# Sandwich layer on eight cores: scores with a 65th row instead of a separate subtraction, K of both heads in rows 0 to 63, and the second LN2 moved

## The chip, the cores and the metric

The program runs on all 8 NeuronCores of one Trainium2 chip, each core on its own half of a sequence. The time is the device time of the slowest core in microseconds (us). TensorE (PE) has two clock levels here, 1.2 and 2.4 GHz; the trace gives the level that was granted as a share of full speed (0.50 or 1.00, a mean in between). DVE is VectorE, ACT is ScalarE, POOL is GpSimd, SP is SyncE, whose queue issues DMAs; PSUM is the memory that PE writes.

## What is computed

One layer of 1024 features on 4 sequences of 4096 tokens: `x = x + LN(attention(LN(x)))`, then `x = x + LN(ffn(LN(x)))`. The attention has 16 heads of 64; q is layer-normalised over all features before it is split into heads, and q is added to the attention's output:

```python
q = layer_norm(x @ Wq + bq, ln_g, ln_b);  k = x @ Wk + bk;  v = x @ Wv + bv
qk = (q * d ** -0.5) . k ;  gmax = max over all keys
out = sum(exp(qk - gmax) v) / (1e-08 + sum(exp(qk - gmax)))      # per head, in key chunks
out = (out + q) @ Wo + bo

h = silu((x @ w1.T) * s1) * ((x @ w2.T) * s2)     # 1024 -> 4096
h = gelu((h @ h1.T) * sh1);  h = gelu((h @ h2.T) * sh2)          # 4096 -> 4096, twice
return (h @ w3.T) * s3                                           # 4096 -> 1024
```

## The kernel before

Each core holds the 4096 tokens of its sequence as keys and 2048 of them as queries. Features lie on partitions, tokens along the free axis. Work is issued in program order on each engine; a small planner (`Prog`) turns declared reads and writes of named buffers into semaphore waits. A buffer name covers a whole tile, so a read waits for the last writer of any part of it.

**A1, A2** (lines 423 to 466) normalise x and project and normalise q. `emit_stats` (386) makes mean and variance with matmuls against ones into the PSUM banks psP1a and psP1b, fed by DVE casts and squares.

**Attention** (648 to 656) loops over 8 head pairs `hp`. `emit_kv` (486) loads two weight slices, makes K for both heads (L506: 8 token chunks of 512, 8 matmuls of 128x128 by 128x512 each; head 0 on partitions 0 to 63, head 1 on 64 to 127) and V (L518, 32 chunks). PSUM banks are dealt out in turn from six slots. Then come 4 query tiles of 512. For each tile, *pass 1* finds the maximum of the scores over all keys for each query: `pass1_steps` makes a list of 68 small steps. Per group of 128 queries (`qs`) there are 16 steps, each one matmul (L539, 64 rows, 512 keys) and one DVE maximum over it (L546), with the bank chosen by the key segment, psP1a for even and psP1b for odd ones, so that the two heads of a segment share a bank. A 17th step reduces the 8 maxima of each head (L554, L557), transposes them on PE (L560) and copies two rows, for head 0 to partition 0 and for head 1 to partition 64 of `grow` (L564, L567).

*Pass 2* (`emit_pass2`, 573) goes over 32 key chunks `kc` of 128. In PE's order each chunk has: the scores of both heads (L595, a pair of 64-row matmuls at tile positions (0, 0) and (64, 0)), the subtraction of the maximum (L602, a pair of 1-row matmuls of -1 by `grow`, accumulated on top), and PV of the chunk before (L582, 65 columns of weights: 64 of V and a column of ones that yields the sum of exponentials). ACT takes exp of both heads at once (L610). Behind that, two steps of pass 1 of the *next* tile are popped. The PSUM banks of scores alternate between psST0 and psST1. After 32 chunks DVE takes two reciprocals (L618, L620), PE spreads them (L622, L625), DVE multiplies and adds q; then the steps that are left over follow. In the last tile of a head pair nothing is popped.

**After attention** the output projection and its LayerNorm (661 to 688) store x1 to DRAM. **FFN** (723 to 864) takes two blocks of 1024 tokens: LN2 of two halves of 512 (L727 load, stats, L734, L736 apply), S1 (w1, w2, silu, product on DVE at L789), h1 and h2 (L811), w3 (L839), final LayerNorm (L855 to L859) and store (L861).

Of the kernel before, what the change touches and what calls it, by code (L numbers as in the profile page):

```python
# [10 lines left out]
AF = mybir.ActivationFunctionType  # L11
# [212 lines left out]
def build_program(cfg):  # L224
# [34 lines left out]
    with stack:  # L259
# [35 lines left out]

        def slot():
            h, lo, b = _slots[_si[0] % len(_slots)]
            _si[0] += 1
            return h[:, lo:lo + 512], b
# [8 lines left out]
        sem_bv = p.dma_sem("bv")  # L308
        sem_big = p.dma_sem("big")
# [27 lines left out]
        o_grow = _o_ws + 4096  # L337
# [16 lines left out]
        b_grow = [p.buf("grow0"), p.buf("grow1")]  # L354
# [31 lines left out]
        def emit_stats(bf_chunks):  # L386
            n = len(bf_chunks)
            for i, (kind, xap, xbufs) in enumerate(bf_chunks):
                if kind == "f32":
                    dst, db = sc16[i % 2], b_sc16[i % 2]  # L390
                    p.op("vector", lambda v, xap=xap, dst=dst: v.tensor_copy(  # L391
                        dst[:, :], xap), reads=list(xbufs), writes=[db], tag="cast")
                    xap, xbufs = dst[:, :], [db]
                sq, bsq = sc16[2 + (i % 2)], b_sc16[2 + (i % 2)]
                p.op("vector", lambda v, xap=xap, sq=sq: v.tensor_mul(sq[:, :], xap, xap),
                     reads=list(xbufs), writes=[bsq], tag="sq")
# [26 lines left out]
        for tc in range(NTC_F if not cfg.get("skip_a1") else 0):  # L423
# [19 lines left out]
            sem_w[0], writes=[b_ws, b_wsV, b_xbs[0], b_xbs[1]] + b_pt + b_grow, tag="wq")  # L443
# [24 lines left out]
        if cfg.get("stop_after_A2"):  # L468
# [3 lines left out]
                              o_pt=o_pt, o_grow=o_grow, o_sc=o_sc, o_ws=o_ws,  # L472
# [8 lines left out]

        kvK = [PB.view(o_ws + i * 128, 128) for i in range(ND)]
# [3 lines left out]
        def emit_kv(hp):  # L486
# [16 lines left out]
            for tc in range(NTC_F):  # L503
                ps, bps = slot()
                for i in range(ND):
                    p.op("tensor", lambda t, i=i, tc=tc, ps=ps: t.matmul(  # L506
                        ps, kvK[i][:, :], xln[i][:, tc * 512:(tc + 1) * 512],
                        start=(i == 0), stop=(i == ND - 1)),
                        reads=[b_ws, b_xln[i]], writes=[bps], war_free=(i > 0), tag="kMM")
                p.op("scalar", lambda s, tc=tc, hp=hp, ps=ps: s.activation(  # L510
                    K_hp[:, tc * 512:(tc + 1) * 512], ps, AF.Identity,
                    bias=bks_t[:, hp:hp + 1], scale=0.125),
                    reads=[bps, bbks], writes=[b_k], tag="kevac")
# [14 lines left out]

        def pass1_steps(hp, qt):
# [3 lines left out]
            steps = []  # L533
            for qs in range(4):
                for seg in range(NSEG):
                    for h in range(2):
                        def th(qs=qs, h=h, seg=seg):
                            pa, pb = (psP1a, bP1a) if (seg % 2 == 0) else (psP1b, bP1b)
                            p.op("tensor", lambda t: t.matmul(  # L539
                                pa[:, :], q_s[c][h * 64:h * 64 + 64,  # L540
                                                 t0 + qs * 128:t0 + (qs + 1) * 128],
                                K_hp[h * 64:h * 64 + 64, seg * 512:(seg + 1) * 512],
                                start=True, stop=True),
                                reads=[b_qs[c], b_k], writes=[pb], tag="s1MM")
# [6 lines left out]
                def th2(qs=qs):  # L551
                    gc0 = o_gc + gsl * 128
                    base = o_cm + gsl * 64 + qs * 16
                    p.op("vector", lambda v: v.reduce_max(  # L554
                        PF.view(gc0, 1), PF.view(base, NSEG), axis=AX.X),
                        reads=[b_cm[gsl]], writes=[b_gc[gsl], b_big1], tag="gA")
                    p.op("vector", lambda v: v.reduce_max(  # L557
                        PF.view(gc0 + 64, 1), PF.view(base + 8, NSEG), axis=AX.X),
                        reads=[b_cm[gsl]], writes=[b_gc[gsl]], tag="gB")
                    p.op("tensor", lambda t: t.transpose(  # L560
                        psP1a[0:65, 0:128], PF.view(gc0, 65), idm_t[:, :]),
                        reads=[b_gc[gsl], bidm], writes=[bP1a], tag="gT")
# [10 lines left out]
        def emit_pass2(hp, qt, nxt):  # L573
# [3 lines left out]
            g0 = o_grow + gsl * 512  # L577
# [12 lines left out]
            for kc in range(NKC):  # L590
# [3 lines left out]
                for h in range(2):  # L594
                    p.op("tensor", lambda t, kc=kc, h=h, pst=pst: t.matmul(  # L595
                        pst[:, h * 512:(h + 1) * 512],
                        K_hp[h * 64:h * 64 + 64, kc * 128:(kc + 1) * 128],
                        q_s[c][h * 64:h * 64 + 64, t0:t0 + 512],
                        start=True, stop=False, tile_position=(h * 64, 0)),
                        reads=[b_k, b_qs[c]], writes=[bsth[h]], tag="stMM")  # L600
                for h in range(2):
                    p.op("tensor", lambda t, h=h, pst=pst: t.matmul(  # L602
# [349 lines left out]
```

How the kernel before makes its waits and increments, by code:

```python
            def body(eng):  # L164
                watermark = {}
                for o in prog.ops[e]:
                    for d in o.deps:
                        if d[0] == "eng":
                            sem = prog.sems[d[1]]
                            val = prog.ops[d[1]][d[2]].sem_val
                            assert val is not None, (d, o.tag)
                        else:
                            sem = d[1].handle
                            val = d[2]
                        key = id(sem)
                        if watermark.get(key, -1) >= val:
                            continue
                        watermark[key] = val
                        eng.wait_ge(sem, val)
                    inst = o.fn(eng)
                    if o.dma_sem is not None:
                        inst.then_inc(o.dma_sem.handle, 16)
                    elif o.inc:
                        inst.then_inc(prog.sems[e], 1)
```

## Time and profile before

| | |
|---|---|
| two timed runs, median | 8107.11 us (8105.29 to 8108.93) |
| profiled execution, time | 8104.53 us |
| its span (first to last instruction, slowest core) | 8103.0 us |
| spans of all cores | 8084.3 to 8103.0 us |
| mean granted clock, cores | 0.688 to 0.691 |
| busy: PE, DVE, ACT, POOL | 5975.2, 2603.2, 1565.0, 641.9 us |
| chain that ended last, by engine | PE 70%, DVE 19%, issue 6%, DMA 3% |

The page is of one profiled execution on the slowest core. Busy times are sums over instructions; PE's are modelled, and overlapping matmuls count together, so the start times of neighbouring matmuls say more than their durations. "x2" in a row of the order of time means that two instructions were merged. In brackets stands how long the engine had been idle before, and whose result ended the wait.

### The profile page before, as it was taken

The page shows a single profiled execution, that of the slowest core. Times are in us where ns is not written, and L with a number is a line of the kernel's source. Part 1 is how long each engine was busy: PE and PEld are TensorE (multiplying, and loading weights), DVE is VectorE, ACT ScalarE, POOL GpSimd, SP SyncE. Part 2 cuts the span into 40 slices and gives each one's busy share as a digit, 9 for nine tenths or more (in the row PEclk, how much of TensorE's full clock was granted, in tenths as well). Part 3 has the DMA queues.
Part 4 walks back from the last instruction along what each step waited for, and adds up shares of the span by engine and source line. Part 5 has one row for each costly group of instructions (what it writes and reads, how often), then busy time and mean ns, then how long its engine had stood idle before and what let it go on. Part 6 is the DMA issues. An engine that isn't in the chain of part 4 may idle for free.

```text
span 8103.0 us, 82459 instructions; the slowest of 8 cores (8084.3 to 8103.0 us)
## 1 busy us (share of the span) xinstructions
PE 5975.2 (74%) x23184; PEld 1921.5 (24%) x23184; DVE 2603.2 (32%) x4355; ACT 1565.0 (19%) x1761; POOL 641.9 (8%) x737
## 2 busy tenths in 40 slices
PE   2456757857757667677677577469999967999995
PEld 0111111211211211111111111124444423444442
DVE  7544344344344344344344443620000023000002
ACT  0212312312212222122122123122001002210000
POOL 0000000000000000000000000001222220122222
PEclk6755555555555555555555555779999988999998
DMA  3100000000000000000000000256877884687888
GB/s 43 13 3 0 1 3 0 2 2 1 3 0 0 3 0 0 3 0 1 3 0 0 11 1 0 79 85 71 79 77 75 80 104 83 73 77 75 78 79 99
DMA packets 781102, 265.62 MB, mean 33 GB/s; under 512 B 684008, under 2 KB 758128, under 8 KB 780656
## 3 DMA queue, kind: packets, MB, share of 16 engines
q0 software_dynamic: 759408, 218.18, 26.7%
q1 hardware_dynamic: 21248, 42.17, 1.5%
q8 instruction: 197, 3.23, 0.2%
q14 instruction: 249, 2.04, 0.1%
HBM read 461.67 MB, written 16.78 MB: 59 GB/s over the span
## 4 chain that ended last, share of the span: by engine, by line
PE 70%; DVE 19%; issue 6%; DMA 3%; ACT 1%; DVEq 1%; POOL 0%; ACTq 0%; POOLq 0%; SPq 0%
PE psST L811 15%; DVE PF L546 10%; PE psPVa L582 7%; PE psST L602 7%; PE psST L595 5%; PE psP1a L539 5%; PE psPVb L582 5%; PE psP1b L539 5%; PE psP1a L811 4%; PE psP1b L811 4%; PE psST L764 2%; PE psST L757 2%; DMA PB<-w3t 2%; PE psST L839 1%; DVE PF L620 1%
## 5 line engine op out<-in xcount | busy, mean ns | idle before, releaser
L610 ACT ACTIVATE PB<-psST 128x1024 bf16<-128x1024 f32 x1024 | 1048.6, 1024 | 3260.3 <-PE psST L602 3259.6
L811 PE MATMUL psST<-PB 128*128 128x512 bf16 x5504 | 1199.4, 380 | 18.1 <-DMA PB<-h1t 18.1
L546 DVE TENSOR_REDUCE PF<-psP1a 128x1 f32<-128x512 f32 x1024 | 708.0, 691 | 927.9 <-PE psP1a L539 364.5
L539 PE MATMUL psP1b<-PB 64*128 64x512 bf16 x1024 | 600.9, 587 | 534.5 <-DVE PF L546 531.1
L546 DVE TENSOR_REDUCE PF<-psP1b 128x1 f32<-128x512 f32 x1024 | 708.1, 692 | 857.7 <-PE psP1b L539 420.8
L539 PE MATMUL psP1a<-PB 64*128 64x512 bf16 x1024 | 598.2, 584 | 497.2 <-DVE PF L546 409.4
L595 PE MATMUL psST<-PB 64*128 64x512 bf16 x2048 | 796.2, 611 | 0.0
L391 DVE CAST PB<-PF 128x512 bf16<-128x512 f32 x128 | 54.9, 429 | 2233.7 <-ACT PF L845 2077.4
L811 PEld LDWEIGHTS psST<-PB 128*128 128x128 bf16 x5504 | 539.6, 98 | 671.0 <-issue 24.4
L582 PE MATMUL psPVa<-PB 128*65 128x512 bf16 x1024 | 644.3, 629 | 5.2 <-ACT PB L610 5.2
L582 PE MATMUL psPVb<-PB 128*65 128x512 bf16 x1024 | 639.1, 624 | 0.0
L602 PE MATMUL psST<-PB,neg_b 1*128 1x512 bf16 x2048 | 615.6, 598 | 10.3 <-DVE PB L567 10.3
L539 PEld LDWEIGHTS psP1b<-PB 64*128 64x128 bf16 x1024 | 102.7, 100 | 994.4 <-issue 994.4
L539 PEld LDWEIGHTS psP1a<-PB 64*128 64x128 bf16 x1024 | 102.6, 100 | 992.8 <-issue 992.4
L818 ACT ACTIVATE PB<-psST,ccol_t 128x512 bf16<-128x512 f32 x172 | 118.3, 688 | 1054.3 <-PE psST L811 1054.2
L811 PE MATMUL psP1a<-PB 128*128 128x512 bf16 x1344 | 296.9, 379 | 0.0
L811 PE MATMUL psP1b<-PB 128*128 128x512 bf16 x1344 | 296.9, 379 | 0.0
L488 POOL DMA_DIRECT2D PB<-wk x8 | 7.0, 876 | 3591.8 <-PE psST L518 1738.8
L602 PEld LDWEIGHTS psST<-PB,neg_b 1*128 1x128 bf16 x2048 | 105.1, 99 | 734.8 <-issue 734.8
L618 DVE RECIPROCAL PF<-psPVa 1x512 f32<-1x512 f32 x32 | 107.4, 3355 | 534.2 <-PE psPVa L582 531.4
L801 POOL DMA_DIRECT2D PB<-h1t x256 | 224.4, 896 | 687.2 <-PE psST L811 421.2
L801 POOL DMA_DIRECT2D PB<-h2t x256 | 224.5, 896 | 659.6 <-PE psST L811 433.1
(129 smaller groups left out, 4435.0 us busy)
## 6 DMA issues: line engine op xcount, KB each, us to landing
PB<-h1t POOLq DMA_DIRECT2D x256, 256.0 KB, 5.8
PB<-h2t POOLq DMA_DIRECT2D x256, 256.0 KB, 5.7
PB<-w3t POOLq DMA_DIRECT2D x128, 256.0 KB, 6.6
PB<-w1t POOLq DMA_DIRECT2D x32, 512.0 KB, 6.2
PB<-w2t POOLq DMA_DIRECT2D x32, 512.0 KB, 8.3
PF<-x1d SPq DMA_DIRECT2D x8, 2048.0 KB, 8.7
PB<-xT POOLq DMA_DIRECT2D x8, 1024.0 KB, 12.0
PF<-xT SPq DMA_DIRECT2D x4, 2048.0 KB, 8.9
```

The costliest lines, as they stand in the source:

```text
L539: p.op("tensor", lambda t: t.matmul(pa[:, :], q_s[c][h * 64:h * 64 + 64, t0 + qs * 128:t0 + (qs + 1) * 128], K_hp[h * 64:h * 64 + 64, seg ...
L546: p.op("vector", lambda v: v.reduce_max(PF.view(col, 1), pa[:, :], axis=AX.X), reads=[pb], writes=[b_cm[gsl], b_big1], tag="s1max")
L582: p.op("tensor", lambda t, kc=kc, h=h, par=par, psv=psv: t.matmul(psv[:, :], V_hp[kc][:, h * 65:h * 65 + 65], PB.t[:, o_pt + par * 1024 + ...
L595: p.op("tensor", lambda t, kc=kc, h=h, pst=pst: t.matmul(pst[:, h * 512:(h + 1) * 512], K_hp[h * 64:h * 64 + 64, kc * 128:(kc + 1) * 128], ...
L602: p.op("tensor", lambda t, h=h, pst=pst: t.matmul(pst[:, h * 512:(h + 1) * 512], neg_b[h * 64:h * 64 + 1, :], PB.t[h * 64:h * 64 + 1, g0:g ...
L610: p.op("scalar", lambda s, par=par, pst=pst: s.activation(PB.t[:, o_pt + par * 1024:o_pt + (par + 1) * 1024], pst[:, :], AF.Exp), reads=bs ...
L618: p.op("vector", lambda v: v.reciprocal(rd[:, 0:512], psPVa[64:65, :]), reads=[bPVa], writes=[b_rd, b_big1], tag="recipA")
L757: p.op("tensor", lambda t, i=i, jj=jj, sb=sb, psa=psa, wi=wi: t.matmul(psa, fsl[wi][:, i * 256 + jj * 128:i * 256 + (jj + 1) * 128], xln2[ ...
L764: p.op("tensor", lambda t, i=i, jj=jj, sb=sb, psb2=psb2, wi=wi: t.matmul(psb2, fsl[2 + wi][:, i * 256 + jj * 128:i * 256 + (jj + 1) * 128] ...
L801: p.dma("gpsimd", lambda g, j2=j2, wi=wi, wt_d=wt_d, jq0=jq0: g.dma_start(PB.view(o_ws + wi * 4096 + jq0 * 128, NJ * 32).rearrange("p (n o ...
L811: p.op("tensor", lambda t, j=j, sb=sb, ps=ps, wi=wi, src=src: t.matmul(ps, PB.view(o_ws + wi * 4096 + j * 128, 128), src[j][:, sb * 512:(s ...
L818: bdst=bdst: s.activation(dst[j2][:, sb * 512:(sb + 1) * 512], ps, AF.Gelu, bias=0.0, scale=cc(scn, j2)),
```

## The change

- **K per head.** The K projection makes 64 columns per matmul group, once per head, and both results lie on partitions 0 to 63: head 0 in `K_hp`, head 1 in two free pieces of the slab (`kb1`, `kb2`). Row 64 of all three is set to 1.0 once.
- **Queries per head.** A first step `th0` of pass 1 copies the 512 queries of head 0 on DVE and moves those of head 1 by a DMA on SP's queue from partitions 64 to 127 to 0 to 63, into tiles `qgv`. The DMA waits for the copy, because both write the buffer `b_qg`.
- **Maximum as a 65th row.** The maxima are stored negated in row 64 of `qgv`. The scores become one 65-row matmul per head, without a tile position; the subtraction matmuls go. Matmuls of pass 1 read rows 0 to 63 for both heads.
- **Transpose step.** It has, per head, a reduction, a transpose and a one-row copy; both heads use the same column of `gc`, head 0 the bank psP1a and head 1 psP1b.
- **LN2 and slots.** LN2 of the second block is emitted behind S1 of the first block, ahead of h1. In the FFN the slots are the four halves of psST0 and psST1.

```diff
...
             for tc in range(NTC_F):
+                for h in range(2):
+                    ps, bps = slot()
+                    for i in range(ND):
+                        p.op("tensor", lambda t, i=i, tc=tc, h=h, ps=ps: t.matmul(
+                            ps[0:64, :], kvK[i][:, h * 64:(h + 1) * 64],
+                            xln[i][:, tc * 512:(tc + 1) * 512],
+                            start=(i == 0), stop=(i == ND - 1)),
...
+            def th0():
+                p.op("vector", lambda v: v.tensor_copy(
+                    qgv[gsl * 2 + 0][0:64, :], q_s[c][0:64, t0:t0 + 512]),
+                    reads=[b_qs[c]], writes=[b_qg[gsl]], tag="qgA")
+                p.dma("sync", lambda sy: sy.dma_start(
+                    qgv[gsl * 2 + 1][0:64, :], q_s[c][64:128, t0:t0 + 512]),
+                    sem_qg[gsl], reads=[b_qs[c]], writes=[b_qg[gsl]], tag="qgB")
+            steps.append(th0)
...
-                                pa[:, :], q_s[c][h * 64:h * 64 + 64,
-                                                 t0 + qs * 128:t0 + (qs + 1) * 128],
-                                K_hp[h * 64:h * 64 + 64, seg * 512:(seg + 1) * 512],
+                                pa[:, :],
+                                qgv[gsl * 2 + h][0:64, qs * 128:(qs + 1) * 128],
+                                rhs, start=True, stop=True),
+                                reads=[b_qg[gsl]] + rbuf, writes=[pb], tag="s1MM")
...
-                    p.op("vector", lambda v: v.reduce_max(
-                        PF.view(gc0, 1), PF.view(base, NSEG), axis=AX.X),
-                    p.op("vector", lambda v: v.reduce_max(
-                        PF.view(gc0 + 64, 1), PF.view(base + 8, NSEG), axis=AX.X),
-                    p.op("tensor", lambda t: t.transpose(
-                        psP1a[0:65, 0:128], PF.view(gc0, 65), idm_t[:, :]),
+                    for h in range(2):
+                        p.op("vector", lambda v, h=h: v.tensor_reduce(
+                            PF.view(gc0 + 64, 1), PF.view(base + h * 8, NSEG),
+                            axis=AX.X, op=ALU.min),
+                            reads=[b_cm[gsl]], writes=[b_gc[gsl], b_big1], tag="gmin")
+                        p.op("tensor", lambda t, pt_=pt_: t.transpose(
+                            pt_[0:65, 0:128], PF.view(gc0, 65), idm_t[:, :]),
+                            reads=[b_gc[gsl], bidm], writes=[bpt_], tag="gT")
+                        p.op("vector", lambda v, h=h, pt_=pt_: v.tensor_copy(
...
+                            reads=[bpt_], writes=[b_qg[gsl]], tag="gcp")
...
-                        start=True, stop=False, tile_position=(h * 64, 0)),
-                        reads=[b_k, b_qs[c]], writes=[bsth[h]], tag="stMM")
-                for h in range(2):
-                    p.op("tensor", lambda t, h=h, pst=pst: t.matmul(
-                        pst[:, h * 512:(h + 1) * 512], neg_b[h * 64:h * 64 + 1, :],
-                        PB.t[h * 64:h * 64 + 1, g0:g0 + 512],
-                        start=False, stop=True, tile_position=(h * 64, 0)),
+                    lhsT, lbuf = k65(h, kc)
+                    p.op("tensor", lambda t, h=h, pst=pst, lhsT=lhsT: t.matmul(
+                        pst[:, h * 512:(h + 1) * 512], lhsT,
+                        qgv[gsl * 2 + h][0:65, :],
+                        start=True, stop=True),
+                        reads=lbuf + [b_qg[gsl]], writes=[bsth[h]], tag="stMM")
...
+        _slot_pool[0] = [2, 3, 4, 5]
...
+        emit_ln2(0)
+        for ft in range(NFT):
...
+            if ft + 1 < NFT:
+                emit_ln2(ft + 1)
             for (wt_d, scn, src, bsrc, dst, bdst) in (
```

## Rows read from the trace of the kernel before

**Rows 1.** The page's first line.
```profile
span 8103.0 us, 82459 instructions; the slowest of 8 cores (8084.3 to 8103.0 us)
```
**Rows 2.** Busy us (instructions) per engine by stretch: K projection, mixed tile, pass 2 alone.
```profile
core 1: us, PE busy (x) PEld busy (x) DVE busy (x) ACT busy (x) POOL busy (x), PEclk, DMA share, GB/s
1008.00:1024.00 16.00, 16.00 (x87) 7.70 (x86) 0.45 (x3) 5.50 (x8) 0.64 (x1) 0.91 0.01 2
...
1160.00:1180.00 20.00, 19.80 (x62) 3.37 (x61) 10.30 (x15) 8.19 (x8) 0.00 (x0) 0.50 0.00 1
...
1512.00:1576.00 64.00, 63.49 (x184) 12.04 (x182) 0.00 (x0) 32.12 (x32) 0.00 (x0) 0.50 0.00 0
```
**Rows 3.** Order of time (start, us, engine, line), pass 2 without pass 1, PE.
```profile
981.55 0.61 PE L595 MATMUL psST<-PB 64*128 64x512 bf16 x2
...
982.63 0.64 PE L582 MATMUL psPVa<-PB 128*65 128x512 bf16 x1
...
983.06 0.63 PE L582 MATMUL psPVb<-PB 128*65 128x512 bf16 x1
983.62 0.61 PE L595 MATMUL psST<-PB 64*128 64x512 bf16 x2
```
**Rows 4.** Order of time, mixed tile, both steps of one segment, PE.
```profile
552.25 0.60 PE L539 MATMUL psP1a<-PB 64*128 64x512 bf16 x1
...
553.86 0.58 PE L539 MATMUL psP1a<-PB 64*128 64x512 bf16 x1 [1.01 <-DVE PF L546]
...
556.33 0.60 PE L539 MATMUL psP1b<-PB 64*128 64x512 bf16 x1
```
**Rows 5.** The same, steps in two banks, at 0.50 and later at 1.00.
```profile
641.61 0.60 PE L539 MATMUL psP1b<-PB 64*128 64x512 bf16 x1
...
644.11 0.60 PE L539 MATMUL psP1a<-PB 64*128 64x512 bf16 x1
...
901.90 0.37 PE L539 MATMUL psP1b<-PB 64*128 64x512 bf16 x1 [0.70 <-DVE PF L546]
...
904.08 0.37 PE L539 MATMUL psP1a<-PB 64*128 64x512 bf16 x1 [0.70 <-DVE PF L546]
```
**Rows 6.** Order of time, start of a K projection, PE.
```profile
1588.74 6.50 PE L506 MATMUL psST<-PB 128*128 128x512 bf16 x16
...
1595.07 1.89 PE L506 MATMUL psP1a<-PB 128*128 128x512 bf16 x8
...
1596.80 1.89 PE L506 MATMUL psP1b<-PB 128*128 128x512 bf16 x8
```
**Rows 7.** Order of time, last transpose step of a tile and its followers.
```profile
1123.28 0.16 DVE L557 TENSOR_REDUCE PF<-PF 128x1 f32<-128x8 f32 x1
1123.59 0.45 PE L560 MATMUL psP1a<-idm_t,PF 128*65 128x128 f32 x1 [1.54 <-DVE PF L557]
...
1124.14 0.28 DVE L564 CAST PB<-psP1a 1x128 bf16<-1x128 f32 x1 [0.70 <-PE psP1a L560]
1124.45 0.29 DVE L567 CAST PB<-psP1a 1x128 bf16<-1x128 f32 x1
1124.89 0.61 PE L602 MATMUL psST<-PB,neg_b 1*128 1x512 bf16 x2 [0.31 <-DVE PB L567]
```
**Rows 8.** DMA issues by line: size and median us from issue to landing.
```profile
onesf_t<-cones SPq DMA_DIRECT2D x1, 64.0 KB, 2.0
```
**Rows 9.** Order of time, FFN: h1's first wait, then the boundary of the blocks.
```profile
5585.14 15.03 PE L811 MATMUL psST<-PB 128*128 128x512 bf16 x62 [8.97 <-DMA PB<-h1t]
...
6656.95 0.38 PE L400 MATMUL psP1b<-PB,ones_b 128*128 128x512 bf16 x1 [0.22 <-DVE PB L395]
...
6683.43 0.38 SPq L861 DMA_DIRECT2D outT<-PF  x1
...
6705.98 0.38 PE L400 MATMUL psP1b<-PB,ones_b 128*128 128x512 bf16 x1 [0.22 <-DVE PB L395]
...
6740.88 0.38 PE L400 MATMUL psP1b<-PB,ones_b 128*128 128x512 bf16 x1 [0.22 <-DVE PB L395]
...
6761.73 3.62 PE L764 MATMUL psST<-PB 128*128 128x512 bf16 x8
```

More of the change, by code:

```diff
@@ L294, in build_program @@
         _si = [0]
+        _slot_pool = [list(range(6))]
         def slot():
-            h, lo, b = _slots[_si[0] % len(_slots)]
+            pool = _slot_pool[0]
+            h, lo, b = _slots[pool[_si[0] % len(pool)]]
             _si[0] += 1
@@ L308, in build_program @@
         sem_bv = p.dma_sem("bv")
+        sem_qg = [p.dma_sem("qg0"), p.dma_sem("qg1")]
         sem_big = p.dma_sem("big")
@@ L336, in build_program @@
         o_pt = _o_ws + 2048
-        o_grow = _o_ws + 4096
+        o_qg = _o_ws + 4096
+        o_kb2 = _o_ws + 6144
+        o_kb1 = _o_sc
+        assert Tf <= 4096
         o_h0 = _main
@@ L353, in build_program @@
         b_pt = [p.buf("ptA"), p.buf("ptB")]
-        b_grow = [p.buf("grow0"), p.buf("grow1")]
+        b_qg = [p.buf("qg0"), p.buf("qg1")]
+        b_kb1, b_kb2 = p.buf("kb1"), p.buf("kb2")
+        qgv = [PB.view(o_qg + i * 512, 512) for i in range(4)]
         b_sc16 = [p.buf(f"sc16_{i}") for i in range(4)]
@@ L395, in emit_stats @@
                 p.op("vector", lambda v, xap=xap, sq=sq: v.tensor_mul(sq[:, :], xap, xap),
-                     reads=list(xbufs), writes=[bsq], tag="sq")
+                     reads=list(xbufs), writes=[bsq, b_kb1], tag="sq")
                 p.op("tensor", lambda t, xap=xap, i=i, n=n: t.matmul(
@@ L503, in emit_kv @@
             for tc in range(NTC_F):
[L504 to L513, printed above, removed]
+                for h in range(2):
[5 more added lines that the diff above has]
+                            start=(i == 0), stop=(i == ND - 1)),
+                            reads=[b_ws, b_xln[i]], writes=[bps], war_free=(i > 0),
+                            tag="kMM")
+                    if h == 0:
+                        dst, dbuf = PB.t[0:64, o_k + tc * 512:o_k + (tc + 1) * 512], [b_k]
+                    elif tc * 512 < 2048:
+                        dst = PB.t[0:64, o_kb1 + tc * 512:o_kb1 + (tc + 1) * 512]
+                        dbuf = [b_kb1] + b_sc16
+                    else:
+                        dst = PB.t[0:64, o_kb2 + tc * 512 - 2048:o_kb2 + (tc + 1) * 512 - 2048]
+                        dbuf = [b_kb2]
+                    p.op("scalar", lambda s, hp=hp, h=h, ps=ps, dst=dst: s.activation(
+                        dst, ps[0:64, :], AF.Identity,
+                        bias=bks_t[h * 64:(h + 1) * 64, hp:hp + 1], scale=0.125),
+                        reads=[bps, bbks], writes=dbuf, tag="kevac")
             for kc in range(NKC):
@@ L721, in _stop, with emit_ln2 @@
             return nc
-        for ft in range(NFT):
+        def emit_ln2(ft):
             tb0 = ft * TB
```

74 lines of the change are left out of this document (41 added, 33 removed).

## The prediction

> **What bounds the kernel now.** I read the page first, then busy time by stretch, then the order of time inside each kind of stretch. The span is 8103.0 us [rows 1]. The profiled execution took 8104.53 us, 1.6 us more than its span, and the two timed runs have a median of 8107.11, so what I add to the span I add to 8107.
>
> Attention fills the span from 425 to about 5071 us, eight head pairs of about 581 us each. There PE decides nearly everything, and mostly at the low one of its two clock levels. In [rows 2] the granted clock is the column behind the engines: 0.91 in the K projection (it starts low and ends at 1.00, 2.4 GHz), but 0.50 (1.2 GHz) in pass 2, although PE is busy for 19.80 of 20 us in one stretch and 63.49 of 64 us in another. ACT has 32 exps in those 64 us, 1.00 us each: half idle. So the clock and the spacing of matmuls are the two things to price.
>
> Three patterns make up pass 2. Alone (query tile 3 of each head pair) one key chunk takes 2.07 us (981.55 to 983.62) [rows 3]: score pair and subtraction pair 1.08, so 0.54 each, PV 0.43, PV 0.56. A 512-column matmul streams 0.43 us here, so the two members of a row-tiled pair run together, and each of three changes of array shape costs 0.11 to 0.13. With the next tile's pass 1 in it, two steps go with each chunk. Where both steps are of one segment they share a PSUM bank, the second waits for the maximum of the first (552.25 to 553.86, 1.61 us), and a chunk takes 4.08 us [rows 4]. Since a group of 16 steps ends with a 17th (the transpose), the pairing shifts, and every other group has its two steps in different banks: 2.50 us at 0.50, 2.18 us at 1.00 [rows 5], where two reductions of 0.69 in a row (10.30 us for 15, [rows 2]) set the pace.
>
> **The change, part by part.**
>
> K projection. 64 matmuls of 128 columns of weights per head pair become 128 of 64; each still streams 512 columns. Before: 16 of them in 6.33 us from a low clock, then 8 in 1.73, that is 0.216 each [rows 6]. If the clock rises as now, the 64 extra cost 64 x 0.216 = 13.8, and with a slightly later rise I take 15.5: 8 x 15.5 = +124 us. If it does not, all 128 take 0.43 (54.7 for about 15.3), and V starts low: +42, times 8 = +336. These are the two ends.
>
> Score and subtraction. Two pairs (four instructions, two array passes) become two separate matmuls of 65 rows, so streaming is the same 0.86, and what goes is the changes of shape: all four matmuls of a chunk now use the full array. At the low clock a chunk alone takes 4 x 0.43 = 1.72 for 2.07: 8 x 32 x 0.35 = -88 us. At the high clock PE needs 0.86 and the loop through exp decides. PV of chunk n waits for exp n, and the scores of n+2 are queued behind it: 0.15 to wake PE (as behind the copy that ends at 1124.74, [rows 7]), 4 x 0.216 + 0.17 for the last to drain, 0.2 to wake ACT (an estimate beside that 0.15), 1.0 of exp, about 2.4 us for two chunks, 1.22 each. With some 6 us before the clock rises a tile takes 42 us for 67: 8 x -25 = -200 us.
>
> Does it rise? No row shows this form. On one side, PE rows are full at 0.50 for 64 us [rows 2], with 65-column PV and three breaks per chunk. On the other, unbroken 512-column matmuls (K projection now) rose within 6.3 us [rows 6], and the denser mixed pattern rose sometimes, as in the high row of [rows 5], and often not in 20 us [rows 2]. The new loop has no break at all, and is therefore nearer to what rises; its half-filled array (65 rows, or 65 columns) is nearer to what doesn't. I take the rise, at 2 in 3. The K projection with 64 columns stands between the same rows.
> The Trainium skill (TensorE: Matmul & The Clock Gate, Part 1) says that the clock follows how busy PE has been, and that only idleness holds it down. By that alone the 64 us stretch should be high already, and the trace disagrees (0.50); for the new loop the rule gives the high clock, and by it the sum is the one below, by the trace's stretch at 0.50 it is the second rival.
>
> Mixed tiles (three per head pair). Pass 1 now reads both heads from rows 0 to 63, so its two matmuls no longer run beside each other, nor beside the score pair. One bank: 1.61, then 0.54, 3 x 0.43, 0.56 = 4.00 (4.08 before). Two banks: 0.43, 0.54, 3 x 0.43, 0.56 = 2.82 (2.50 before). The new first step th0 shifts the pairing: of 32 chunks 14 share a bank (16 before), 14 don't (13), 4 are special (3). Before: 65.3 + 32.5 + 12 (what is left of the loop's 110 us). After: 56.0 + 39.5 + 18.6 = 114, the specials being 3.0 for the first chunk, 5.5 twice and 4.6 once (below). So +4 in the loop.
>
> The transpose step. It was reduction, reduction, one transpose, two copies, 1.30 us from transpose to the next matmul [rows 7]. Now each head has its own reduction, transpose and copy in one chain through one column buffer: after the first copy (0.55 after its transpose starts, 0.28 long) come 0.1, 0.16, 0.15, 0.55, 0.28 and 0.15, less the reduction (0.26) and the copy (0.31) that move into it, +0.66. The next s1 matmul, or the scores, wait for the last copy, since they read the same buffer; before, the score pair ran under the copies. So +0.66 at three and +1.3 at the last of each tile. Behind each mixed tile five steps are left over instead of four, one more bank wait, 1.6: with the transpose +2.9. Mixed tiles: 24 x 6.9 = +166 us.
>
> th0: a 64x512 copy (0.2 to 0.4) and a 64 KB transfer. The nearest row, 64 KB on the same queue, lands in 2.0 us [rows 8]. The s1 matmul behind it waits, and behind that in PE's order the next chunk. At a mixed tile it starts with the scores, so 1.45 us show (that is in the 3.0). Ahead of a head pair it queues behind the last V evacuations on DVE and shows in full, 3.4 us by estimate. With its transposes (3 x 0.66 + 1.3) the first pass 1 costs 6.7: 8 x 6.7 = +54 us. SP has nothing else due there; if the copy found DVE behind, each us late is 24 us in all.
>
> Clock in the mixed tiles. The two-bank stretches are denser than before, so more of them should rise. Each rise gives 0.62 us over some 5 chunks until the next transpose idles PE; half of 48 stretches: 24 x 3.1 = -74, less 8 that the present rises already give: -66.
>
> FFN. The second LN2 moves ahead of h1. In PE's order its matmuls come where h1 now starts 9 us after S1 ends: casts and first half 8.5 us, then 34.9 to the end of the second half (6705.98 to 6740.88) [rows 9], so h1 starts at about +43.5: +35 us. At the later boundary PE now goes from 6656.95 to 6761.73 before it is dense again [rows 9]; S1 could start at 6657, would stop after some 7 us since its products queue on DVE behind the block's last normalisation (to 6683.43), and run on from about 6684: -80 us. Together -45. Four slots for six hide behind 3.5 us of matmuls per pair. The memsets once: +5.
>
> Sum: 124 + 54 + 166 - 200 - 66 - 45 + 5 = +38, or 8145 us.
>
> **Rivals.** (1) K low, pass 2 high: 38 + 212 = +250, about 8360, or 8420 with no rises in the mixed tiles. For it: 64-column weights fill half the array, as PV does where the clock stays low. (2) Both low: 336 + 54 + 166 - 88 - 45 + 5 = +428, 8535. For it: the 64 us at 0.50 [rows 2]. Against: those have breaks, this has none. (3) K high, pass 2 low: 8323. (4) Faster: once risen, the clock holds through the transposes and the one-bank stretches, where a chunk would take 2.7 us for 4.0 (1.4 between its two steps, then 0.32, 3 x 0.216, 0.33): 14 x 1.3, 11 x 0.62 and 3 for the specials are 28 a tile, 24 x -28 = -672 in place of the -66, about 7540. It decides from the point where the high clock survives the first transpose step, in which PE waits some 3 us. Against: the high stretches of pass 2 that I followed in the trace ended at such a wait or at the reciprocals. The change does do what it says: both matmul forms and the order are fixed in the code.
>
> **Numbers.** Forecast 0.50, its own range 8075 to 8215 (K 15 to 18 us, th0 1 to 3 us, none or all of the 149 us that a rise in every two-bank stretch gives). Rivals: (2) 0.25, (1) 0.11, (3) 0.07, (4) 0.07. Range 8060 to 8560: it holds all but (4) and the edges, 8 in 10. Two per cent is 162 us, about what can be told from no change here: faster 0.07, same 0.49, slower 0.44.
>
> **What would show it.** Right: granted clock 1.00 in the K projection and in the tile without pass 1, chunks at about 1.22 there, 4.0 and 2.8 in mixed tiles, two transposes in series, S1 of the second block starting right behind the first block's W3. Wrong: 0.50 in K (54 us), 1.72 us chunks at 0.50, or one-bank chunks near 2.7.

## The result, and the profile after

The changed kernel takes 8190.89 us (median of 18 runs, 8174.65 the lowest) beside 8138.37 (median of 17, 8105.29 the lowest) for the kernel before: a ratio of 1.0079, interval 1.0058 to 1.0100. It is slower, by less than the 2% that I had set as the bound, and within the forecast's own range of 8075 to 8215. Medians of all eight-core runs hold some in which one die runs at a lower clock; ratios, and what is compared below, leave these runs or that die out.

The profiled execution of after took 8190.84 us. Page of after: span, busy time by engine, granted clock in 40 slices.
```profile
span 8189.3 us, 80850 instructions; the slowest of 8 cores (8157.6 to 8189.3 us)
...
PE 6039.1 (74%) x21533; PEld 2131.4 (26%) x21776; DVE 2631.3 (32%) x4391; ACT 1600.7 (20%) x1826; POOL 642.7 (8%) x737
...
PEclk6765565565655655755655655869999998999997
```
The span answers to [rows 1]. The 6s and 7s at even distances in the first three quarters are the head pairs' K projections and tiles without pass 1; the 5s between them are the rest of attention, at the low level.

Core 1 can be compared in both traces (8103.0 and 8175.9 us). I split it at the starts of its instructions (the loop of a tile ends at its first reciprocal); each time is a sum over the head pairs, in us.

| stretch (times it occurs) | before | after | difference | forecast |
|---|---|---|---|---|
| start to the first head pair | 425.0 | 447.5 | +22.5 | +5 |
| K, V and th0, up to the first s1 matmul (8) | 257.9 | 391.4 | +133.5 | +151 |
| first pass 1 (8) | 690.8 | 719.2 | +28.4 | +27 |
| loops of the mixed tiles (24) | 2660.2 | 2715.0 | +54.8 | +30 |
| what follows them: left-over steps, reciprocals (24) | 419.6 | 497.2 | +77.6 | +70 |
| tile without pass 1 (8) | 537.6 | 328.5 | -209.1 | -200 |
| tail of a head pair (8) | 96.7 | 95.4 | -1.3 | 0 |
| behind attention | 3015.0 | 2981.7 | -33.3 | -45 |
| sum | 8102.8 | 8175.9 | +73 | +38 |

The forecast column is that of the prediction, regrouped: 124 of K and 27 of th0; 8 x 3.3 of transposes; 96 less 66 for the loops; 24 x 2.9.

Busy time by stretch, core 0 of after; the granted clock stands behind the five engines. A tile without pass 1, a stretch with steps in two banks, one with steps in one bank, a K projection.
```profile
core 0: us, PE busy (x) PEld busy (x) DVE busy (x) ACT busy (x) POOL busy (x), PEclk, DMA share, GB/s
994.00:1028.00 34.00, 27.48 (x112) 9.15 (x110) 0.52 (x1) 27.33 (x28) 0.00 (x0) 1.00 0.00 1
725.00:740.00 15.00, 15.00 (x34) 3.34 (x32) 7.61 (x12) 5.50 (x6) 0.00 (x0) 0.50 0.00 0
616.00:648.00 32.00, 23.57 (x50) 5.83 (x49) 11.27 (x19) 8.18 (x8) 0.00 (x0) 0.50 0.00 0
1052.00:1066.00 14.00, 14.00 (x66) 7.15 (x65) 0.00 (x0) 5.45 (x8) 0.00 (x0) 1.00 0.01 2
```
The first row answers to the last of [rows 2]: 0.50 before, 1.00 now. The second is the one that I had wrong: PE is busy for 15.00 of 15 us and stays at 0.50, where I expected every other such stretch to rise. On no core of after does a mixed tile rise.

Order of time in the tile without pass 1 (start, length, engine, line), core 0 of after, ahead of the rise and well behind it.
```profile
991.47 1.06 PE L646 MATMUL psST<-PB 65*128 65x512 bf16 x2
993.17 0.75 PE L646 MATMUL psST<-PB 65*128 65x512 bf16 x2
...
1015.46 1.94 ACT L653 ACTIVATE PB<-psST 128x1024 bf16<-128x1024 f32 x2 [0.41 <-PE psST L646]
...
1016.63 0.38 PE L632 MATMUL psPVa<-PB 128*65 128x512 bf16 x1 [0.41 <-ACT PB L653]
...
1017.81 1.94 ACT L653 ACTIVATE PB<-psST 128x1024 bf16<-128x1024 f32 x2 [0.41 <-PE psST L646]
```
A chunk takes 1.70 us at 0.50 (991.47 to 993.17; forecast 1.72). At 1.00, ACT's two exps and its wait of 0.41 repeat every 2.35 us (1015.46 to 1017.81), 1.17 a chunk (forecast 1.22): the loop through exp decides there, as worked out. A tile takes 41.06 us for 67.20.

Mixed tiles, pass-1 matmuls of core 0 of after: two banks, then one bank.
```profile
598.27 0.63 PE L591 MATMUL psP1a<-PB 64*128 64x512 bf16 x1
...
600.66 0.61 PE L591 MATMUL psP1a<-PB 64*128 64x512 bf16 x1
601.06 0.63 PE L591 MATMUL psP1b<-PB 64*128 64x512 bf16 x1
...
622.16 0.60 PE L591 MATMUL psP1a<-PB 64*128 64x512 bf16 x1
623.77 0.58 PE L591 MATMUL psP1a<-PB 64*128 64x512 bf16 x1 [1.01 <-DVE PF L597]
...
626.11 0.60 PE L591 MATMUL psP1b<-PB 64*128 64x512 bf16 x1
```
Two banks: 598.27 to 601.06, 2.79 us (2.50 in [rows 5]; forecast 2.82). One bank: 622.16 to 626.11, 3.95 (4.08 in [rows 4]; forecast 4.00), with the same 1.61 between its two steps: the wait for the maximum, 1.01, is untouched by the change.

The last transpose step of a first pass 1, and th0 of the next tile, core 0 of after.
```profile
582.69 0.45 PE L612 MATMUL psP1a<-idm_t,PF 128*65 128x128 f32 x1 [1.29 <-DVE PF L606]
583.24 0.29 DVE L615 CAST PB<-psP1a 1x128 bf16<-1x128 f32 x1 [0.70 <-PE psP1a L612]
583.56 0.16 DVE L606 TENSOR_REDUCE PF<-PF 128x1 f32<-128x8 f32 x1
583.87 0.45 PE L612 MATMUL psP1b<-idm_t,PF 128*65 128x128 f32 x1 [0.73 <-DVE PF L606]
584.49 0.29 DVE L615 CAST PB<-psP1b 1x128 bf16<-1x128 f32 x1 [0.77 <-PE psP1b L612]
584.81 0.29 DVE L578 COPY PB<-PB 64x512 bf16<-64x512 bf16 x1
584.93 1.01 PE L646 MATMUL psST<-PB 65*128 65x512 bf16 x2 [0.61 <-DVE PB L615]
585.17 0.46 SPq L581 DMA_DIRECT2D PB<-PB  x1
587.17 0.58 PE L591 MATMUL psP1a<-PB 64*128 64x512 bf16 x1 [1.23 <-DMA PB<-PB]
```
The chain is the one forecast, link by link: transpose, copy, reduction, transpose, copy. It takes 2.24 us from the first transpose to the scores, 2.22 by the forecast's links; in [rows 7] the scores start 0.38 behind the transpose and the subtraction 1.30. The transfer of th0 lands 2.0 us after its issue, and PE waits for it.

### The profile page after: what moved, and what is told of

It reads as the page before. It is cut to its first block, busy times and chain, and to the rows that moved or that the text cites. A ratio compares the mean times of both kernels' runs of the same rounds, so it can differ in the third digit from the quotient of the medians.

```text
span 8189.3 us, 80850 instructions; the slowest of 8 cores (8157.6 to 8189.3 us)
## 1 busy us (share of the span) xinstructions
PE 6039.1 (74%) x21533; PEld 2131.4 (26%) x21776; DVE 2631.3 (32%) x4391; ACT 1600.7 (20%) x1826; POOL 642.7 (8%) x737
## 4 chain that ended last, share of the span: by engine, by line
PE 67%; DVE 18%; issue 7%; DMA 4%; ACT 2%; DVEq 1%; ACTq 0%; POOL 0%; SPq 0%; POOLq 0%
PE psST L861 21%; PE psST L646 10%; DVE PF L597 9%; PE psP1a L591 6%; PE psP1b L591 6%; PE psPVa L632 5%; PE psPVb L632 4%; PE psST L812 3%; PE psST L805 3%; PE psST L889 2%; PE psST L524 2%; DMA PB<-w3t 2%; ACT PB L653 2%; DVE PF L663 1%; PE psST L546 1%
## 5 line engine op out<-in xcount | busy, mean ns | idle before, releaser
L861 PE MATMUL psST<-PB 128*128 128x512 bf16 x8028 | 1763.5, 380 | 26.5 <-DMA PB<-h1t 17.9
L861 PEld LDWEIGHTS psST<-PB 128*128 128x128 bf16 x8192 | 802.0, 98 | 987.6 <-issue 24.7
L646 PE MATMUL psST<-PB 65*128 65x512 bf16 x2048 | 963.8, 570 | 19.9 <-DVE PB L615 19.9
L591 PE MATMUL psP1b<-PB 64*128 64x512 bf16 x1024 | 620.6, 606 | 382.6 <-DVE PF L597 382.6
L632 PE MATMUL psPVa<-PB 128*65 128x512 bf16 x1024 | 590.1, 576 | 48.2 <-ACT PB L653 45.2
L632 PE MATMUL psPVb<-PB 128*65 128x512 bf16 x1024 | 589.9, 576 | 0.0
L868 ACT ACTIVATE PB<-psST,ccol_t 128x512 bf16<-128x512 f32 x256 | 175.9, 687 | 1588.3 <-PE psST L861 1588.3
L889 PE MATMUL psST<-PB 128*128 128x512 bf16 x1004 | 256.3, 419 | 84.1 <-DMA PB<-w3t 82.7
L646 PEld LDWEIGHTS psST<-PB 65*128 65x128 bf16 x2048 | 164.1, 112 | 537.4 <-issue 486.1
L805 PE MATMUL psST<-PB 128*128 128x512 bf16 x1001 | 244.8, 383 | 34.0 <-ACT PB L830 17.0
L632 PEld LDWEIGHTS psPVa<-PB 128*65 128x65 bf16 x1024 | 166.0, 162 | 378.0 <-issue 378.0
L812 PE MATMUL psST<-PB 128*128 128x512 bf16 x1006 | 242.7, 382 | 2.3 <-DMA PB<-w2t 1.4
```

Of the source, the lines that this page charges most:

```text
L591: p.op("tensor", lambda t, rhs=rhs, qs=qs, h=h: t.matmul(pa[:, :], qgv[gsl * 2 + h][0:64, qs * 128:(qs + 1) * 128], rhs, start=True, stop= ...
L632: p.op("tensor", lambda t, kc=kc, h=h, par=par, psv=psv: t.matmul(psv[:, :], V_hp[kc][:, h * 65:h * 65 + 65], PB.t[:, o_pt + par * 1024 + ...
L646: p.op("tensor", lambda t, h=h, pst=pst, lhsT=lhsT: t.matmul(pst[:, h * 512:(h + 1) * 512], lhsT, qgv[gsl * 2 + h][0:65, :], start=True, s ...
L805: p.op("tensor", lambda t, i=i, jj=jj, sb=sb, psa=psa, wi=wi: t.matmul(psa, fsl[wi][:, i * 256 + jj * 128:i * 256 + (jj + 1) * 128], xln2[ ...
L812: p.op("tensor", lambda t, i=i, jj=jj, sb=sb, psb2=psb2, wi=wi: t.matmul(psb2, fsl[2 + wi][:, i * 256 + jj * 128:i * 256 + (jj + 1) * 128] ...
L861: p.op("tensor", lambda t, j=j, sb=sb, ps=ps, wi=wi, src=src: t.matmul(ps, PB.view(o_ws + wi * 4096 + j * 128, 128), src[j][:, sb * 512:(s ...
```

## The experiments

**1. The bank of a pass-1 step, in the kernel before.** The one-bank wait was there before and after. This takes it away, by choosing the bank by head:
```
-pa, pb = (psP1a, bP1a) if (seg % 2 == 0) else (psP1b, bP1b)
+pa, pb = (psP1a, bP1a) if (h == 0) else (psP1b, bP1b)
```


> The kernel before, with one edit: pass 1 takes its PSUM bank by head (psP1a for head 0, psP1b for head 1) and not by key segment, so that no two neighbouring steps share a bank. Theory (the wait in a mixed chunk is the bank shared by the two steps, not the clock and not DVE): the 16 chunks per mixed tile that take 4.08 us take 2.50, and the pair of steps in the first pass 1 of a head pair goes from 2.39 to about 1.65 us; 24 x 25 us and 8 x 24 us less, about 7310 us, granted clock still mostly 0.50 in pass 2 (some rises). Rival (DVE is the limit and the wait only moves): mixed chunks stay near 4 us, over 8000 us.

Measured: ratio 0.8885, interval 0.8796 to 0.8973; the profiled execution took 7247.88 us. First pass 1 takes 61.35 us for 86.3, a mixed tile 84.57 for 110.84. Pass-1 matmuls of core 0:
```profile
644.85 0.61 PE L539 MATMUL psP1a<-PB 64*128 64x512 bf16 x1
647.34 0.60 PE L539 MATMUL psP1b<-PB 64*128 64x512 bf16 x1
647.35 0.61 PE L539 MATMUL psP1a<-PB 64*128 64x512 bf16 x1
649.84 0.60 PE L539 MATMUL psP1b<-PB 64*128 64x512 bf16 x1
```
At 0.50 every chunk now takes 2.50 us, as only the two-bank ones did. The two members of a pair start together, and no maximum is waited for. Some of the gain is clock: 17 of the 24 mixed tiles of core 0 have a stretch at 1.00, 205 us in all, for 82 us in the kernel before; its slowest tile takes 88.2 us, the mean is 84.57 (81.2 on core 6, which has 416 us at 1.00). One word of the code is worth about 11% (the lowest runs, 7247.88 against 8108.14, give 0.894), more than the whole change under study moved in either direction. The tile without pass 1 still takes 67.20 us at 0.50.

**2. The same edit in the kernel after.**


> The changed kernel with the same edit (bank by head). Theory: one-bank chunks of 3.95 us become two-bank chunks of 2.79 us, 24 x 14 x 1.16 = 390 us less, and the first pass 1 of a head pair loses 8 x 24 us: about 7610 us, so that the changed kernel then stands some 4% behind the kernel before with the same edit, since its matmuls of pass 1 and the scores no longer run in pairs (2.79 for 2.50 us a chunk). Rival: with the long waits gone the clock rises in the mixed tiles (chunks near 2.2 us or less), under 7450 us.

Measured: its lowest run is 7556.43 us, with all cores between 7536 and 7555; in the profiled execution core 0 (7542.1 us) has first pass 1 516.6, mixed loops 2330.7 (97.11 a tile), tiles without pass 1 327.6. It gains 620 where before gained 860, and stands 4.3% behind experiment 1. That gap is the change without the cover of the bank wait: a chunk of 2.79 instead of 2.50 everywhere, the longer transpose step, K, and the stretches at 1.00, which the mixed tiles of experiment 1 have and these don't; the tiles without pass 1 give 210 us back. Although PE now waits less, no mixed tile rises.

**3. FFN part alone, in the kernel before:** four slots for six, and the second block's LN2 behind S1 of the first.
```
+        emit_ln2(0)
         for ft in range(NFT):
...
+            if ft + 1 < NFT:
+                emit_ln2(ft + 1)
```


> The kernel before with the FFN part of the change alone: LN2 of the second block behind S1 of the first, and four PSUM slots in the FFN. Theory from the two traces: 25 to 30 us less (the span behind attention was 3010 us and became 2984). Rival (the forecast's term): 45 us less. A second rival, that the move only shifts the wait: no change.

Measured: ratio 0.9923, interval 0.9859 to 0.9987. What lies behind attention takes 2958 to 2970 us by core for 3003 to 3015: -45, what the prediction said, and not the 25 to 30 that I expected here. In after the same stretch takes 2972.5 to 2997.8, so some of it is lost there. On the slowest cores, 0 and 5, PE waits for h1t twice, 17.6 to 17.9 us for 8.5 on core 1; the waits for w3t (80.7 to 89.7 us by core) don't sort the cores. What makes the transfers later wasn't tried. Core 1 of after shows both halves of the term:
```profile
5728.90 0.58 PE L406 MATMUL psP1a<-PB,ones_b 128*128 128x512 bf16 x1 [29.00 <-DVE PB L400]
...
5737.49 7.71 PE L861 MATMUL psST<-PB 128*128 128x512 bf16 x35
...
6814.48 0.38 PE L409 MATMUL psP1b<-PB,ones_b 128*128 128x512 bf16 x1 [0.22 <-DVE PB L404]
6814.72 1.89 PE L805 MATMUL psST<-PB 128*128 128x512 bf16 x8
...
6842.20 3.57 PE L805 MATMUL psST<-PB 128*128 128x512 bf16 x8 [16.96 <-ACT PB L830]
```
h1 starts at 5737.49, 49 us behind the end of S1, 9 in [rows 9]: +40 for the +35 of the sum. And S1 of the second block starts straight behind W3, stops for 16.96 us on its products, and runs on, as forecast. The forecast's -80 for that boundary is small by its own rows (104.8 us less the 20 of the stop is 85), which with +40 gives the same -45.

**4. K in halves of 64 columns alone, in the kernel before.**
```
-                ps, bps = slot()
+                for h in range(2):
+                    ps, bps = slot()
...
-                        ps, kvK[i][:, :], xln[i][:, tc * 512:(tc + 1) * 512],
+                        ps[0:64, :], kvK[i][:, h * 64:(h + 1) * 64],
```


> The kernel before with the K projection alone changed: 64 columns of weights per matmul, once per head, 128 matmuls per head pair for 64. Theory (64 more matmuls at the high clock, 0.216 us each): 8 x 14 to 15.5 = 110 to 125 us more, granted clock 1.00 in K as in the changed kernel. Rival (the clock stays low with half the array filled): 8 x 40 = 320 us more.

Measured: ratio 1.0123, interval 1.0021 to 1.0225; K and V take 371.3 us for 257.9, +113, and no other stage moves by more than 5 us. By head pair 14.2 us, for 64 matmuls at 0.216 = 13.8. The clock reaches 1.00 with weights of 64 columns: my first rival is refuted by itself here.

**5 and 6. Does PV's half-filled array hold the clock down?** PV's weights widened from 65 to 128 columns (the added result rows are not used), in the kernel before and in the kernel after.
```
-                        psv[:, :], V_hp[kc][:, h * 65:h * 65 + 65],
+                        psv[0:128, :], PB.t[:, o_v + kc * 130 + h * 65:o_v + kc * 130 + h * 65 + 128],
```


> The kernel before, but PV's weights are 128 columns wide instead of 65 (the columns behind the 65th are neighbouring V data and their result is not read). The order, the shapes in rows and the breaks between matmuls stay. Theory A (how much of the array a matmul fills counts for the clock): pass 2 without pass 1, 0.50 for its whole length before, rises, and a chunk takes less than 1.5 us for 2.07. Theory B (only the breaks of 0.11 to 0.13 us at a change of array shape hold the clock down): the clock stays at 0.50 there and chunks stay at 2.07 us.

> The changed kernel with PV 128 columns wide. Its mixed tiles stayed at 0.50 in all stretches, even where PE streams 2.58 of 2.79 us. Theory A (fill counts): the two-bank stretches of the mixed tiles rise at least sometimes, as they did in the kernel before. Theory B (only breaks count): they stay at 0.50, as in the changed kernel. In the tile without pass 1 both expect 1.00 and 1.17 us a chunk.

Measured, before with it (core 2, 8089.4 us): a tile without pass 1, and a K/V stage.
```profile
core 2: us, PE busy (x) PEld busy (x) DVE busy (x) ACT busy (x) POOL busy (x), PEclk, DMA share, GB/s
944.00:984.00 40.00, 40.00 (x120) 6.60 (x118) 0.00 (x0) 20.31 (x20) 0.00 (x0) 0.50 0.00 1
1022.00:1046.00 24.00, 24.00 (x264) 18.62 (x262) 11.11 (x54) 3.44 (x5) 0.87 (x1) 0.81 0.12 12
```
PE is busy for 40.00 of 40 us, PV fills all columns, and the clock is 0.50; a tile without pass 1 takes 66.4 us for 67.2. After with it: cores 4 and 5 took 8160 and 8167 us, mixed tiles 113.17 each, none risen. So the width of PV is not what differs between the stretches at 0.50 and those at 1.00. The 0.81 in the second row is taken up at the end.

**7. The transpose step in parallel, in the kernel after:** each head has a column buffer of its own; both reductions, both transposes, both copies.
```
-b_gc = [p.buf("gc0"), p.buf("gc1")]
+b_gc = [p.buf(f"gc{i}") for i in range(4)]
```


> The changed kernel with a column buffer of its own for each head in the transpose step: both reductions, then both transposes, then both copies. Theory (the serial chain through one column buffer costs what the prediction said, 0.66 us of waiting at 128 steps, somewhat less where other work covers it): 50 to 85 us less than the changed kernel, about 8100. Rival (the second transpose costs by itself and not by the chain): under 25 us less.

Measured: 8069.15 us, cores 8033 to 8068 for 8158 to 8189, about -120. By stage: first pass 1 690.8 (-28), mixed loops 2646.7 (-68), what follows them 476.0 (-21). One step, core 1:
```profile
607.04 0.45 PE L612 MATMUL psP1a<-idm_t,PF 128*65 128x128 f32 x1 [1.28 <-DVE PF L607]
...
607.31 0.45 PE L612 MATMUL psP1b<-idm_t,PF 128*65 128x128 f32 x1
...
607.55 1.06 PE L647 MATMUL psST<-PB 65*128 65x512 bf16 x2
607.66 0.29 DVE L616 CAST PB<-psP1a 1x128 bf16<-1x128 f32 x1 [0.50 <-PE psP1a L612]
```
The transposes follow each other by 0.27 us for 1.18 to 1.25, and the scores behind them start 0.51 us after the first, for 1.42 to 1.49 in after. The prediction priced the serial step at 3 x 0.66 + 1.3 = 3.28 a tile, 105 us for 32 tiles; the three stages give 118, 3.7 a tile. My expectation for this run was lower than that, 50 to 85, and wrong: I had allowed for cover by other waits that isn't there.

**8. th0's second half by a DVE copy instead of a transfer, in the kernel after.**
```
-                p.dma("sync", lambda sy: sy.dma_start(
-                    qgv[gsl * 2 + 1][0:64, :], q_s[c][64:128, t0:t0 + 512]),
-                    sem_qg[gsl], reads=[b_qs[c]], writes=[b_qg[gsl]], tag="qgB")
+                p.op("vector", lambda v: v.tensor_copy(
+                    qgv[gsl * 2 + 1][0:64, :], q_s[c][64:128, t0:t0 + 512]), ...
```


> The changed kernel, with the queries of head 1 brought to partitions 0 to 63 by a second DVE copy (0.29 us) instead of the DMA on SP's queue. Theory (the DMA's landing is on PE's path, as the 61.4 us that PE sat idle for PB<-PB say): 45 to 60 us less than the changed kernel. Rival (DVE, or the exp behind it, is late there anyway): under 20 us less.

Measured: 8134.22 us, cores 8102 to 8133, about 55 below those of after; K, V and th0 -15.3 (1.9 a head pair), mixed loops -32.2 (1.3 a tile). The transfer was on the path in both places.

**9. One K projection of 128 columns, evacuated in two halves, in the kernel after.** The score matmuls keep their form.
```
-                        ps[0:64, :], kvK[i][:, h * 64:(h + 1) * 64],
+                        ps, kvK[i][:, :],
...
-                        dst, ps[0:64, :], AF.Identity,
+                        dst, ps[h * 64:(h + 1) * 64, :], AF.Identity,
```


> The changed kernel with the K projection undone: 64 matmuls of 128 columns per head pair as in the kernel before, and two evacuations that put each head's half on partitions 0 to 63. Theory (the K term is real and stands alone): 8 x 14 to 16 = 110 to 130 us less than the changed kernel, about 8060. Rival (ACT's two evacuations per bank, or the clock, take part of it back): under 80 us less.

Measured: 8071.39 us; K, V and th0 282.8 to 286.5 by core for 391.0 to 393.1, -105 to -110, 13.1 to 13.7 a head pair, just under what I expected. ACT moves the upper 64 rows of the product to rows 0 to 63 with no loss that shows. So the 512 extra matmuls bought nothing.

**10. Why does no mixed tile rise?** After two experiments the columns were out; what was left were the rows. Scores over 128 rows in place of 65, rows 65 to 127 of both operands filled with zeros once, in the kernel after:
```
-                return PB.t[0:65, o_k + kc * 128:o_k + (kc + 1) * 128], [b_k]
+                return PB.t[0:128, o_k + kc * 128:o_k + (kc + 1) * 128], [b_k]
...
-                        qgv[gsl * 2 + h][0:65, :],
+                        qgv[gsl * 2 + h][0:128, :],
```


> The changed kernel with scores over 128 rows: rows 65 to 127 of K and of the queries are zero and are multiplied along; the result is the same and so are the number, length and order of matmuls. Theory C (how many rows of the array the scores fill counts for the clock): the two-bank stretches of the mixed tiles, always 0.50 in the changed kernel and still 0.50 with PV at 128 columns, rise, 24 x 6 to 9 us less (150 to 220 us), or up to 680 us if the clock then holds through the one-bank stretches. Theory D (only the breaks between array shapes count, of which the scores have as many as before): no change but +9 us of memsets.

Measured (cores 4 to 7, 7981 to 8012 us, for 8160 to 8188 in after; the lowest run took 8017.40 us): the mixed loops take 2524.2 us for 2715.0, 105.18 a tile. Core 6, a two-bank stretch, then a one-bank stretch:
```profile
core 6: us, PE busy (x) PEld busy (x) DVE busy (x) ACT busy (x) POOL busy (x), PEclk, DMA share, GB/s
607.00:617.00 10.00, 6.89 (x28) 2.00 (x26) 6.45 (x10) 5.11 (x5) 0.00 (x0) 1.00 0.00 0
625.00:655.00 30.00, 21.96 (x46) 5.26 (x44) 10.34 (x18) 8.18 (x8) 0.00 (x0) 0.50 0.00 0
```
```profile
608.17 0.37 PE L597 MATMUL psP1b<-PB 64*128 64x512 bf16 x1 [0.62 <-DVE PF L603]
...
610.35 0.37 PE L597 MATMUL psP1a<-PB 64*128 64x512 bf16 x1 [0.62 <-DVE PF L603]
```
Every two-bank stretch rises, all 48 on each of cores 4 to 7, and then takes 2.18 us a chunk; each falls back at a transpose step or in the one-bank stretch behind it. Nothing was added to what is computed or to the number of instructions in the loop, only rows of zeros. Ahead of the rise the two kernels can't be told apart by how busy PE is. The first two-bank stretch of a mixed tile on core 6, in after and then with the rows of zeros:
```profile
588.50:603.00 14.50, 14.45 (x32) 3.04 (x32) 6.42 (x10) 6.38 (x7) 0.00 (x0) 0.50 0.00 0
```
```profile
599.00:603.00 4.00, 3.94 (x9) 0.86 (x10) 1.41 (x3) 2.29 (x3) 0.00 (x0) 0.50 0.00 0
603.00:610.00 7.00, 5.36 (x21) 1.50 (x19) 4.61 (x7) 3.62 (x4) 0.00 (x0) 1.00 0.00 0
```
In after PE is busy for 14.45 of 14.50 us (3.95 of the first 4.00) and stays at 0.50; with 128 rows it is busy for 3.94 of 4.00 and goes to 1.00.

**11 and 12. All of it together.** Both kernels are after with the bank by head, parallel transposes, th0 by copies and the whole K projection; the second also has the rows of zeros.

> The last kernel without its zero rows: the scores over 65 rows as in the changed kernel, all else as in the run before (bank by head, a column buffer per head, th0 by two copies, whole K projection). Theory C (rows filled by the scores count for the clock): the mixed tiles stay mostly at 0.50 and chunks near 2.79 us, about 7290 us, so that the 63 rows of zeros alone are worth some 700 us. Theory D (the clock rises there because the long waits are gone): within 2% of the run before, 6600 to 6700.

> All that the runs pointed to, on the changed kernel: bank by head, a column buffer per head, th0 by two copies, whole K projection, and scores over 128 rows. Without any rise of the clock in the mixed tiles the terms add to about 7290 us (7556 for bank by head, less 110, 115 and 50, and 9 for memsets). Under theory C the mixed chunks go from 2.79 to some 1.65 us, where two reductions of 0.79 set the pace: 24 x 30 us less, about 6600.

Measured: 65 rows, ratio 0.8890, interval 0.8794 to 0.8986 (lowest run 7285.32). 128 rows, ratio 0.7983, interval 0.7954 to 0.8012 (lowest 6571.93): the best kernel of the study, 19 to 20% below the one before (the lowest runs, 6571.93 against 8105.29, give 0.811, and 7285.32 with 65 rows gives 0.899). Core 0 of each, 20 us inside the second mixed tile of the first head pair:
```profile
700.00:720.00 20.00, 19.34 (x43) 4.59 (x43) 9.63 (x17) 7.16 (x7) 0.00 (x0) 0.50 0.00 0
```
```profile
640.00:660.00 20.00, 17.47 (x66) 5.65 (x65) 15.03 (x26) 11.22 (x11) 0.00 (x0) 1.00 0.00 0
```
The first is the kernel with 65 rows: PE is busy for 19.34 of 20 us, at 0.50. The second is the one with 128: 17.47, at 1.00, with half as much again done. The mixed loops take 2236.3 and 1508.7 us (62.86 a tile), 728 apart. The other stages of attention agree within 4 us; the start (10 us more, the larger memsets) and what lies behind attention (22 us more, cause not followed) take the difference of the spans to 695. DVE is busy for 15.03 of those 20 us, two reductions a chunk of 0.69, and mostly sets the pace now.

## Why the prediction was right, and where it was not

The forecast was 8145 us for 8190.89, class "within 2%", from the likeliest case. Against the profiled spans the sum says +38 and the trace +73 (core 1) to +86 (slowest cores). That it came so near is in part luck: the terms below miss by up to 66 us, in both directions. By its steps:

- **K projection high:** right. 1.00, and 14.2 (experiment 4) to 14.8 us a head pair (what is left of the stage after th0) for 15.5. -17 with th0.
- **Tile without pass 1 rises:** right, on every core, in every head pair: 41.06 for 42 forecast. This was taken at 2 in 3 by a comparison with no row of its form; the argument I gave for it, that no change of array shape is left, was never tried alone. Rows alone don't decide it either: with 65 rows this loop is high, and the mixed one, with pass 1's matmuls of 64 rows between them, is low until the scores fill 128.
- **th0:** right in kind; ahead of a head pair 1.9 us over a copy, and 1.3 at a mixed tile for 1.45.
- **Transpose steps:** right in their order, somewhat low in size: the first pass 1 grows by 3.55 us a tile for 3.28. The three steps inside a tile cost 0.69 for 0.66 (from the last s1 matmul to the next, 3.42 us before and 4.11 after). The last costs 1.60 up to the scores (2.50 and 4.10) for 1.3: before, the scores started ahead of the copies and only the subtraction waited 0.31 for them.
- **Loop of a mixed tile:** 2.79 and 3.95 for 2.82 and 4.00. 14 x 3.95 + 14 x 2.79 + 18.6 = 113.0, and a tile took 113.13. Before was estimated at 110 and took 110.84, with its few rises in it: +2.3 a tile for +4.
- **Rises in the mixed tiles, -66:** wrong, and the one step that failed. There were none on any core. The step took the high stretches of before as a property of density ("the two-bank stretches are denser than before, so more of them should rise"), and the denser stretch didn't rise once on eight cores. What the runs show in its place is the rows (experiments 10 to 12): with scores over 65 rows none of these stretches rises, over 128 rows all of them do. The loops without it were forecast at +96 and the trace has +55, so 41 of the 66 us don't show in the sum: the answer was nearer than the step deserved. The other 25, the start (17), FFN (12) and the transposes (9 with the left-over steps), less 17 for K and th0, 9 for the tiles without pass 1 and 1 for the tails, are the way from +38 to +73.
- **FFN:** -45 alone in the kernel before (experiment 3), -33 in after on core 1, -7 to -10 on cores 0 and 5.
- **Start, +5:** +22.5 on core 1. The one-row memsets with their waits are some 9 us of it: 3.47 us for 4096 elements in one partition, twice 1.76 for 2048. The rest is a spread of the stages ahead of them, in which I see no cause.

One number of the rivals is off by its own rows: K takes 6.33 + 48 x 0.216 = 16.7 us and not 15.3, so a low clock there would cost 41 and not 42 a head pair. Of the rivals, (1), (2) and (3) needed a low clock in K or in the tile without pass 1 and fell with the windows above. (4), the clock that survives the transposes, did not happen in after. But the last experiment is that case: once the bank waits are gone, the transposes are parallel and the rows are full, the clock holds at 1.00 for 50 us at a time (640 to 690 us on core 0), and 6572 us is below the 7540 that I gave for it.

The Trainium skill (TensorE: Matmul & The Clock Gate, Part 1) lets the clock follow how busy PE has been. The prediction weighed it with [rows 2] against it. It comes out no better behind: the kernel with 65 rows has PE busy for 19.34 of 20 us in a mixed tile and stays at 0.50, as did the 40.00 of 40 us of experiment 5, and in experiment 10 the same order of matmuls rises or not by the rows alone.

What stays open: whether the rows that the scores fill act through the array's activity or in another way. No run varied them between 65 and 128, and none widened pass 1's 64 rows. In the kernel before, the row-tiled pairs fill 128 rows between them, with one-row pairs beside them. Its mixed tiles rise now and then (10 of 24 on core 1), and with the bank by head in 17 of 24 (core 0), where the 65-row kernel with the same bank has no rise: that speaks for the rows too, but none of the runs separates the pairs from the rest. All rows were filled by zeros, so what the same edit does with other data isn't known.

## What to carry to other kernels

Before a structure is rewritten for the clock, look for the wait that ends last in the same loop: here a choice of bank by segment instead of by head cost about 11%, and the rewrite around it moved 1%. A stretch in which PE is all but always busy can still be at 1.2 GHz; read the granted clock beside the busy time, and when it is 0.50, the same matmuls over full rows, with zeros, are a cheap thing to try: they gave 2% here with the bank waits in place and 10% without them. A chain that is made serial by one shared small buffer (a column, 128 floats) costs its length in every tile: 118 us here for 32 tiles.

## What was not expected of the hardware

- Zeros in rows 65 to 127 of the score matmuls are worth some 700 us of 7285: granted clock 0.855 for 0.727 as a mean over the kernel.
- PV over 128 columns instead of 65 changes neither the clock nor, by much, the time of a tile without pass 1 (in after 41.11 us for 41.06, in the kernel before 66.4 for 67.2).
- There is a level beside the two named at the start: the K/V stage of some cores of experiment 5 was granted 0.81, 24 us with PE busy 24.00, and took 34.5 to 35.1 us instead of 32. It doesn't come with the wide PV: in experiment 6 cores 4 to 7 have the wide PV and none of it, and cores 0 to 3 of experiment 10 have it without (425 to 1006 us of each). The Trainium skill (TensorE: Matmul & The Clock Gate, Part 1) lists a state of 13/16 of the full clock, a limit on current, beside the two levels; the trace's 0.81 agrees with that figure. That a current limit is the cause is not shown here.
- A DVE copy of 64x512 bf16 from partitions 64 to 127 down to 0 to 63 takes 0.29 us; the same 64 KB by a transfer cost 1.3 to 1.9 us on the path.
- A memset of 4096 bf16 elements in one partition takes 3.47 us, while one of 128x256 in f32 takes 0.27: in these two the elements per partition count, not their total.
